# Three dense graph sums in one kernel: the fourteen tiles per sum that were gathered row by row are multiplied by counts like the others

## The reference, cut to what matters

```python
def _sage_conv(x, src, dst, Wl, bl, Wr, n_nodes):      # layer 0, used twice: conv1 and conv2
    msgs = x[src]
    agg = jax.ops.segment_sum(msgs, dst, num_segments=n_nodes)
    deg = jax.ops.segment_sum(jnp.ones(src.shape[0], x.dtype), dst, num_segments=n_nodes)
    mean = agg / jnp.maximum(deg, 1.0)[:, None]
    return mean @ Wl.T + bl + x @ Wr.T
...
norm = dinv[src] * dinv[dst]                            # layer 3, K = 3 hops
h = x
for _ in range(K):
    h = jax.ops.segment_sum(norm[:, None] * h[src], dst, num_segments=n)
return h @ W + b
```

## Time and profile before

| | us |
|---|---|
| time, median of 3 runs | 7796.58 |
| lowest and highest run | 7790.68, 7798.47 |
| span of the profiled execution, first to last instruction | 9801.1 |
| TensorE busy in the profiled execution | 5741.5 |
| GpSimd busy in it | 4415.5 |
| VectorE busy in it | 3083.8 |

### The profile page before, as it was taken

How to read it: one execution, slowest core, us unless ns; L and a number is a source line. 1 busy time by engine, 2 the same in 40 slices (tenths; PEclk the granted TensorE clock), 3 DMA queues, 4 the chain that set the end, 5 groups by cost and what they waited for, 6 DMA issues and landing times.

```text
span 9801.1 us, 162158 instructions
## 1 busy us (share of the span) xinstructions
PE 5741.5 (59%) x61597; PEld 4880.9 (50%) x61597; DVE 3083.8 (31%) x5282; ACT 1323.5 (14%) x1657; POOL 4415.5 (45%) x4340
## 2 busy tenths in 40 slices
PE   6999767744444334435653455555455556766777
PEld 6999557732322222224542344444444445666677
DVE  6999211121111111115832333233232332211111
ACT  4777200000000000003630000000000000000000
POOL 2111043346666666666606555555555543333332
PEclk9999878866666666667955666666666677887888
DMA  4444245532232233325701222222222235655555
GB/s 133 181 183 184 88 142 180 186 106 76 81 85 77 77 81 80 81 76 158 212 25 23 69 75 75 74 75 70 67 76 75 75 87 169 194 182 176 179 181 171
DMA packets 615168, 1123.56 MB, mean 115 GB/s; under 512 B 208638, under 2 KB 420608, under 8 KB 601872
## 3 DMA queue, kind: packets, MB, share of 16 engines
q1 hardware_dynamic: 226560, 727.34, 23.1%
q10 hardware_dynamic: 253712, 248.81, 8.0%
q0 software_dynamic: 134432, 140.53, 7.2%
HBM read 857.78 MB, written 258.51 MB: 114 GB/s over the span
## 4 chain that ended last, share of the span: by engine, by line
PE 28%; issue 26%; another core or an unknown queue 17%; PEld 5%; DVE 5%; DMA 2%; POOL 2%; ACT 1%; DVEq 1%; SPq 0%; ACTq 0%; PEldq 0%; POOLq 0%
PE banks L885 11%; PE banks L1040 9%; PEld banks L885 5%; PE banks L1050 4%; POOL gath L383 1%; DVE oneh L1101 1%; PE banks L563 1%; DVE area L1926 1%; DMA area<-edge_h 1%; PE banks L575 1%; DVE oneh L1935 1%; PE banks L555 0%; PE banks L1636 0%; DMA near_rows<-wide 0%
## 5 line engine op out<-in xcount | busy, mean ns | idle before, releaser
L383 POOL DMA_INDIRECT gath<-tab_l,idx x3328 | 3152.2, 947 | 2581.1 <-issue 1076.0
L915 POOL DMA_INDIRECT wide<-near_rows,kept x798 | 845.6, 1060 | 1873.3 <-PE banks L895 1125.7
L1636 PE MATMUL banks<-area,ones 128*128 128x448 f32 (+1 forms) x1040 | 617.0, 764 | 1095.6 <-DVE area L1926 959.1
L1040 PE MATMUL banks<-area 128*128 128x128 f16 x4802 | 581.4, 248 | 905.3 <-issue 904.5
L1636 PEld LDWEIGHTS banks<-area,ones 128*128 128x128 f32 x1040 | 288.1, 289 | 1413.7 <-issue 1400.5
L1040 PEld LDWEIGHTS banks<-area 128*128 128x128 fp8e4 x4802 | 359.7, 108 | 1107.1 <-issue 1102.5
L1050 PE MATMUL banks<-oneh,gath 128*64 128x128 f32 x3328 | 593.7, 358 | 386.1 <-DMA gath<-tab_l,idx 330.2
L1926 DVE TENSOR_TENSOR area<-gath,banks 128x448 f32<-128x448 f32 (+1 forms) x256 | 138.6, 583 | 2049.7 <-remote 1951.3
L1050 PEld LDWEIGHTS banks<-oneh,gath 128*64 128x64 f32 x3328 | 556.1, 191 | 417.9 <-DMA gath<-tab_l,idx 335.2
L885 PE MATMUL banks<-wide,gath 128*128 128x128 f16 x8232 | 574.3, 234 | 208.7 <-issue 189.0
L848 ACT CAST wide<-banks 128x784 uint16<-128x784 f32 x784 | 651.1, 858 | 222.8 <-PE banks L805 222.8
(11 more groups left out here) (261 smaller groups left out, 6643.8 us busy)
## 6 DMA issues: line engine op xcount, KB each, us to landing
gath<-counts SPq DMA_DIRECT2D x252, 784.0 KB
oneh<-counts SPq DMA_DIRECT2D x252, 784.0 KB
counts<-wide SPq DMA_DIRECT2D x98, 1568.0 KB, 5.2
gath<-counts ACTq DMA_DIRECT2D x98, 784.0 KB
area<-counts ACTq DMA_DIRECT2D x98, 784.0 KB
area<-edge_feat SPq DMA_DIRECT2D x128, 448.0 KB
gath<-tab_l,idx POOLq DMA_INDIRECT x3328
edge_h<-area ACTq DMA_DIRECT2D x128, 416.0 KB
```

What stands on the lines that cost most here:

```text
L383: pool.indirect_dma_start(out=to[:, h, c, 0:H], out_offset=None, in_=table[:, :], in_offset=bass.IndirectOffsetOnAxis(ap=idx[:, slot, c:c ...
L915: pool.indirect_dma_start(out=pick_rows[k][r][:, c, :], out_offset=None, in_=near_rows[k][:, :], in_offset=bass.IndirectOffsetOnAxis(ap=pi ...
L1040: last = T.matmul(to, part_in[u].bitcast(f8)[:, t, s * P:(s + 1) * P], block_rows[:, k % 2, s, :, :].rearrange("p a f -> p (a f)"), start= ...
L1636: ins = T.matmul(bank[n][:, 0:(hi - lo) * H], ones[:, :], src[:, lo:hi, :].rearrange("p c f -> p (c f)"), start=first and lo == 0, stop=la ...
```

## The change

All 14 tiles of a round are summed from counts. The picked tiles are gone with everything that served them: the 42 gathers of 19 DMAs, the one-hots, the row tables and their stores, the run search and its lists, the second semaphore of each consumer, and the kept lists in SBUF.

```diff
-PICKS, CHUNKS = (TB - 1, 2 * TB - 1), 19
-RUN = CHUNKS * P
-PICKED = [2 * TB * i + t for i in range(DITERS) for t in PICKS]
-DENSE = [t for t in range(2 * TB) if t not in PICKS]
-NP_PAIR, ND_PAIR = len(PICKS), len(DENSE)
+ND_PAIR = 2 * TB
...
         def counts_in(sp, k, each=None):
             def block_of(i, h):
-                for o, t in enumerate(DENSE):
-                    if t // TB != h:
-                        continue
-                    u, g = o % 2, ND_PAIR * i + o
+                for t in range(h * TB, (h + 1) * TB):
+                    u, g = t % 2, ND_PAIR * i + t
...
-        def either_product(pe, k, i, t, to, of, end):
-            if t in DENSE:
-                product(pe, k, i, t, to, of, end)
-            else:
-                picked_product(pe, k, i, PICKS.index(t), to, end)
...
         def times_counts(pe, k, src):
-            pe.sem_inc(p_near[k].summed, NP_PAIR)
...
-                    either_product(pe, k, i, t, to, parts[src], False)
+                    product(pe, k, i, t, to, parts[src], False)
...
             with dve.Fori(0, DITERS) as i:
                 for t in range(2 * TB):
-                    if t % TB == 0:
-                        picked_onehot(dve, k, i, t // TB)
                     tile(i, t)
...
-                    if j > 0:
-                        act.wait_ge(f_lo, j)
-                        block_out(act, 1, j - 1, parts[1])
-            if k == EARLY:
-                act.wait_ge(f_lo, NB)
-                block_out(act, 1, NB - 1, parts[1])
...
-                act.wait_ge(y_top, 9)
-                act.dma_start(near_rows[0].rearrange("(t p) c -> p t c", p=P), rows2.rearrange("p t a f -> p t (a f)"))\
-                    .then_inc(g_tab, 16)
...
-            dve.wait_ge(g_fit, 1)
...
-            V.tensor_tensor(ok_i[:, :], chk[0:1, 1:2], chk_n[:, 1:2], ALU.mult).then_inc(s_ok_in, 1)
+            V.tensor_copy(ok_i[:, :], chk[0:1, 1:2]).then_inc(s_ok_in, 1)
...
             def both_parts(k):
                 def work(b, h):
-                    n = (b - h) // 2 * ND_PAIR + sum(t // TB <= h for t in DENSE)
-                    hold(dve, h_mm[k], 2 * n + 4)
-                    hold(dve, p_near[k].summed, b + 1 + NP_PAIR)
+                    hold(dve, h_mm[k], 2 * TB * (b + 1) + 4)
```

More of the change, by code:

```diff
@@ L89, in gnn_program @@
         counts = dram("counts", [NT, P, NT * P // 4])
-        near_rows = [nc.dram_tensor(f"near_rows{k}", [NP, 2 * H], f16, kind="Internal").ap() for k in range(3)]
         degree_row = dram("degree_row", [1, NP])
@@ L498, in halves, with turns @@
             return [t[lo:hi, h, j * HB:(j + 1) * HB] for j in range(2)]
-        def turns(eng, d, steps, place=lambda step: step, period=None, beside=()):
+        def turns(eng, d, steps, place=lambda step: step, period=None):
             period = period or d.steps
@@ L507, in turns @@
             late = [(place(step) + lag - period, 1, 1, step, work) for step, work in steps if place(step) + lag > period]
-            own = [(at, 2, 0, None, work) for at, work in beside]
             def run(i, parts):
                 for _, h, back, step, work in sorted(parts, key=lambda part: part[:2]):
-                    if step is None:
-                        work(i)
-                        continue
                     d.wait(eng, i - back, h, step)
@@ L523, in run @@
                         done(ins, d, h)
-            run(0, even + odd + own)
+            run(0, even + odd)
             with eng.Fori(1, DITERS) as i:
-                run(i, even + odd + late + own)
+                run(i, even + odd + late)
             run(DITERS, late)
@@ L1339, in _ @@
             with pool.If(ok > 0):
-                pool.wait_ge(g_list, 32 * len(PICKED))
-                picked_in(pool, 0)
                 edges_to_sums_pool(pool, n_win, 1, 0, early=True)
-                for k in (1, 2):
-                    picked_in(pool, k)
             with pool.Else():
@@ L1489, in _ @@
                 early_act(act, EARLY, EARLY, GROUPS)
-                with act.Fori(0, DITERS) as i:
-                    for h in range(2):
-                        hold(act, h_dve[0], 4 * TB * (2 * i + h + 1))
-                        block_out(act, 2, 2 * i + h, parts[0])
                 turns(act, d_out, [(7, take_feat), *ln_act(10)], LAST_AT.get, DENSE_PERIOD)
@@ L1546, in _ @@
             T.matmul(bank[6][0:1, P:2 * P], chk[:, 1:2], ident, start=True, stop=True).then_inc(s_ok_in, 1)
-            pe.wait_ge(b_find, 13)
-            T.matmul(bank[5][0:BATCHES, 0:P], found[:, 2, :], ident, start=True, stop=True).then_inc(g_fit, 1)
-            pe.wait_ge(g_fit, 3)
-            for n in range(2):
-                for q in range(4):
-                    at = P + (4 * n + q) * BATCHES
-                    last = T.matmul(bank[5][0:1, at:at + BATCHES], found[0:BATCHES, n, q:q + 1],
-                                    ident[0:BATCHES, 0:BATCHES], start=True, stop=True)
-            last.then_inc(g_fit, 1)
             def mlp_by_feat(b, h):
@@ L1621, in work @@
                                      start=True, stop=False)
-                        either_product(pe, k, (b - h) // 2, TB * h + t, to, of, k == 0)
+                        product(pe, k, (b - h) // 2, TB * h + t, to, of, k == 0)
                 return work
@@ L2096, in _ @@
             with dve.If(ok > 0):
-                dve.wait_ge(g_list, 32 * len(PICKED))
-                for m, j in enumerate(PICKED):
-                    V.tensor_scalar(pick_dst[:, m, :], pick_raw[:, m, :], float(j * P), None, ALU.subtract).then_inc(g_list, 1)
-                V.tensor_copy(iota_h, iota0).then_inc(g_list, 1)
-                dve.wait_ge(g_list, 33 * len(PICKED) + 1)
                 turns(dve, d_dense, [(4, both_parts(0)), (5, to_mean), (6, plus_resid), *ln_dve(7), (13, ln_scale(1)),
                                      (19, plus_row(d_dense, 3, R_B1)), (20, clear_padding)],
-                      DENSE_AT.get, DENSE_PERIOD, beside=onehots_beside(dve, 0))
+                      DENSE_AT.get, DENSE_PERIOD)
                 dve.wait_ge(s_deg, 32)
@@ L2111, in _ @@
                 turns(dve, d_out, [(4, both_parts(2)), (5, last_scaled), (9, lambda b, h: add_resid(b, h, 3)),
-                                   *ln_dve(10), (16, result_d)], LAST_AT.get, DENSE_PERIOD,
-                      beside=onehots_beside(dve, 2))
+                                   *ln_dve(10), (16, result_d)], LAST_AT.get, DENSE_PERIOD)
             with dve.Else():
```

83 lines of the change are left out of this document (3 added, 80 removed).

## The result

The changed kernel took 7958.14 us (median of 4 runs, 7952.23 to 7964.54). The kernel before took 7793.63 us beside it (4 runs). The ratio is 1.0215, with a 95% interval of 1.0203 to 1.0227, and the medians differ by 164.5 us. The forecast was +152.4 us and 7949 us.

A forecast was written before the change was run, and what follows sets the result against it. The prediction took TensorE at full clock to bound stages 0 to 2 in the timed runs. Its terms, 185.2 - 30.0 - 2.8 = +152.4 us on the timed median, gave 7949 us, with an 8-in-10 range of 7880 to 8010.

The forecast's parts named there:

- The case called likeliest: Stages 0 to 2 bound by TensorE, timed runs free of crawl: 7949 us, own range 7885 to 7975, chance 0.80.
- Term 1: Stages 0 to 2: 42 picked tiles become counted ones, each about 4.41 us longer on TensorE, nothing hiding it: +185.2 us.
- Term 2: Stage 0: TensorE's wait for the first pick's gather goes, with its slow restart: -30.0 us.
- Term 3: Between build and MLP: VectorE's search of runs goes, one small operation remains: -2.8 us.
- Terms 4 and 5: VectorE's one-hots and the row-table stores go, both beside TensorE's work: zero, at most -84 and -7 us.
- Term 6: SP loads 14 tiles instead of 12 per round; transfers keep up, gathered rows no longer share engines: 0 to -43 us.
- Case C: Transfers become the bound at 278 GB/s, a counted tile taking 5.78 us: 8006 us, chance 0.05.
- the crawl: TensorE's single matmuls 0.4 to 2 us apart around GpSimd's gathers; put at 2047 us of the profile, none in timed runs.
- Case A: The crawl is in the timed runs too; stages 0 to 2 lose 741 us, about 7056 us, chance 0.12.
- The rule weighed in the prediction: Improve the most contended engine; the change adds 3318 matmuls to TensorE, already busiest, so +185 us against the change.

The follow-up runs named there:

- Experiment 11: Kernel before with all 14 tiles of a round counted, but row tables, gathers, one-hots and TensorE's waits for them kept: 7989.93 us, ratio 1.0266.
- experiment 5: Kernel before with gathers of picked rows replaced by a GpSimd fill, and no row tables or waits for them: 7746.71 us, ratio 0.9953.
- experiment 12: The kernel before without gathers or row tables, buffers filled by GpSimd, run again in another series: 7752.57 us, ratio 0.9956.
- experiment 8: Kernel before with TensorE's rounds of the three stages written out and the two picks of stage 0's first round counted: 7677.82 us, ratio 0.9862.
- experiment 1: The kernel before, unedited, profiled again: 7788.75 us, ratio 1.0005; profile span 7782.7 us.
- experiment 9: The changed kernel again, unedited, in a series where the kernel before takes 9910.58 us: 9251.04 us, ratio 0.9335.
- experiment 10: Changed kernel with two rounds in each pass of TensorE's loops, 6 jumps back instead of 16; kernel before 9910.58 us beside it: 9186.12 us, ratio 0.9270.
- the third series: The changed kernel unedited and with two rounds per loop pass, beside the kernel before: 9251.04, 9186.12 and 9910.58 us.

## Why the prediction was right, and where it was not

The case called likeliest came true: 7958 against 7949 us, inside its own range. Term by term:

- **Term 1 (+185.2).** The size is right where TensorE runs without a seam: written out, the three stages take 156 us more after the change than before, and with the 30 us of term 2 put back that is 4.43 us for each of 42 tiles. The looped kernels take 178.5 us more in the same stages. The other 22 us are what the seams cost more after than before, 101 - 79; of these 14 are longer stands (64.6 us against 50.2), the rest lies in the slower tiles behind them. That is the missing term. Experiment 11 has term 1 with the seams on top: 202.5 us (196 to 218 by the interval).
- **Term 2 (-30.0).** Right in mechanism and size. Without gathers stage 0 is 23 and 28 us shorter (experiments 5 and 12), and experiment 8 gives 20.4 + 8.8 = 29.2 us in it. The whole times fall by more, -35.7 and -34.8 us, and by 25.4 + 8.8 = 34.2 us in experiment 8; what lies beyond stage 0 is within the intervals of some 10 us and is given no cause. (One figure in the term's reasoning is off: by the earlier trace rows a gather takes (285.9 + 77.1) / 14 = 25.9 us, not 24. It fits beside six tiles all the same.)
- **Term 3 (-2.8).** Stage 0's first product starts at 1178.0 in the changed kernel and at 1183.3 in the kernel before of experiment 1, 1181.8 in the earlier trace rows: -3.7 to -5.3 us. The sign is safe and the size is not: over all traces it starts at 1178.0 to 1178.7 without the search and at 1180.0 to 1185.4 with it.
- **Terms 4 and 5 (0).** Right by experiment 11, in stages 1 and 2 to 2 us.
- **Term 6 (0 to -43).** Transfers kept up (285 GB/s with TensorE busy for 543.74 of 546 us), and the gathers gave nothing back. Case C did not occur. The working calls the second window of the earlier trace rows gapless, but it shows TensorE busy for 17.95 of 20 us. The missing 2 us are the first part of a seam's stand of 3.21 us, which ends at 8287.16. So a seam lay in the rows that the working rests on.

The change costs 12.1 us more than the 152.4 forecast. The seams add 22 us to it; the other 10 us, the other way, lie outside the three stages or in the scatter of runs, and no experiment assigns them. That the two nearly halve each other is luck. The sum 202.5 - 35 - 3 = 164.5 us from experiments 11 and 5 meets the result more closely than it can be trusted to, since the first two terms have intervals of some 10 us each.

Of what the changed profile would show, the seventh tile at once came true, and GpSimd's absence. The span of 9060 us, the distance of 1110 us to the median and the crawl in the long stretches did not, in the series of the result. They did in kind in that of experiments 9 and 10: 9242.6 us of span, long stretches of 2488 and 2955 us.

**The step that failed in its reason** is the sentence "I take the crawl to be something that the profiled execution has and the timed runs have not". It held for the timed runs shown: they had no crawl. The 2047 us it worked out are near the 2018 us by which the first trace is longer than that of experiment 1. They met the 2004.5 us in part by luck, since its 899 us in the stages hold some 79 us of seams that timed runs have too, and the 1148 us in the long stretches are 24 too few. But the cause is not profiling. Eleven of the fourteen traces, from series where the kernel before takes 7.78 to 7.79 ms, have no crawl. In the third series all timed runs have it as well. Most likely the prediction compared a trace taken under that condition with times taken without it. The clock of 0.741 and the lengths of the stages and stretches speak for it, but no timed run is on record beside that trace. Case A, given 0.12, is what happens there: -659.5 us. It was worked out as -741 us in the stages; the traces give -637 us. The seams of the changed kernel (101 us), missing there too, are most of the difference. The rule weighed in the prediction (the Trainium skill, Perfetto Trace Analysis, § Identifying Performance Opportunities) thus agrees with the result, where the added matmuls cost their price, and the bare rows of the first trace with the third series.

Still open: what the condition is (the chip, a core of it, a neighbour's work or where the series places its data; no run separates them), and whether under it GpSimd's gathers alone make TensorE crawl in the stages. The rows speak for the gathers (the crawl lies only where GpSimd issues them, and it left the stages with them). But the experiments meant to separate gathers from picked products met a series without a crawl.

## What to carry to other kernels

When the profiled execution and the timed runs differ by a quarter, first take a new trace in another series: the two may not be of the same condition, and a change can be 2% slower in one and 7% faster in the other. Replacing a sparse path by a dense one cost its matmuls at full price here, where TensorE is the bound, and what served the sparse path beside TensorE gave nothing back but the wait it had caused. And a loop whose body is some thousands of TensorE instructions is worth writing out before its products are touched: here that was 79 us (1%) with the same products, and a counted first round another 25 us.

## What the runs showed of the hardware

**Each jump back of these loops costs TensorE 2.7 to 5.0 us of standing and part of a tile's pace.** The stands are as many as the jumps in every looped trace of the experiments (16, or 6 in experiment 10), and the written-out ones have none. The granted clock was 0.97 in the changed kernel's stage 0 and 1.00 with the rounds written out; a tile behind a seam took 7.95 us for 5.47. A round here has 14 x 98 matmuls, each with its weight load, and with the loops written out the engine ran through the same instructions with no stand. In every stand a packet of instructions comes in, and TensorE goes on 1.2 to 2.1 us after it. The Trainium skill, Runtime: NRT & Kernel Launch, § Instruction fetch mechanics, says that TensorE's instruction memory holds 2048 instructions, is refilled in blocks of 256, and is prefetched sequentially, and that a taken branch to an instruction outside the part held there has to wait for a fetch of it. A jump back over 2744 instructions would then find nothing there, and the packets in the stands and the 16 KB packets saved agree. That the stand is the wait for this fetch rests on these times; no run slows or speeds the fetch alone. Advanced Engine Details and Errata, § Control Flow Timing, of the Trainium skill gives some 51 ns for a branch; the 4.41 us measured at the seam are far from it.

**A condition in which TensorE crawls while GpSimd issues indirect DMAs.** It held for a whole series, in every run of three kernels, and was gone 16 minutes later. The kernel before took 9910.58 us in it and 7782 to 7794 us in the other comparisons. Within that series it lay where GpSimd gathers: the three stages without gathers agree to 2 us with those of the other series. That the gathers cause it is not shown, as said above.
